# Bilinear stage of a two-layer graph network: the sixteen products of a tile stored term by term instead of value by value

## The reference, cut to what matters

```
node = h @ W1                              # h = layernorm(x), 4096x128; W1: 128x16
hw = jnp.einsum('nc,kcf->nkf', h, W2)      # W2: 16x128x128
x = jnp.einsum('nk,nkf->nf', node, hw)     # 16 terms summed, weighted per row
x = adj @ x
x = x + node @ b
return jax.nn.relu(x)
```

## Time and profile before

| what | us |
|---|---|
| runs of the kernel before, median of 3 | 2064.73 (2064.36 to 2067.2) |
| the profiled execution's own time | 2066.36 |
| its span in the trace | 2064.6 |
| the loop over the 32 tiles, from the first product to the end of the last sum | 1561.0 to 1657.2 |
| busy in the span: TensorE, VectorE, ScalarE, GpSimd | 1814.2, 1639.6, 1351.9, 203.1 |
| mean granted TensorE clock over the span | 0.921 of full speed |

### The profile page before, as it was taken

One profiled execution on the slowest core, in us unless ns is written; L12 is line 12 of the kernel. 1 busy time (PEld: TensorE's weight loads), 2 busy tenths in 40 slices (PEclk: granted clock), 3 DMA queues, 4 the chain that ended last, 5 costly groups with the idle time before them and its releaser, 6 DMA issues.

```text
span 2064.6 us, 28345 instructions
## 1 busy us (share of the span) xinstructions
PE 1814.2 (88%) x8959; PEld 877.8 (43%) x9108; DVE 1639.6 (79%) x1427; ACT 1351.9 (65%) x1498; POOL 203.1 (10%) x158
## 2 busy tenths in 40 slices
PE   1531969999999999999997999999998889997997
PEld 1521434444444444444446444444453344454443
DVE  7655669888989898989566787777858988856997
ACT  6876148887887887887244556555546877735775
POOL 0000000000101011001450000000006900000000
PEclk6555989999999999999996999999989999988999
DMA  9996066555555556455400311101002089913221
GB/s 385 411 421 223 32 204 204 152 152 173 151 151 172 152 152 180 143 153 157 170 0 1 105 52 41 51 34 47 1 21 122 0 327 428 421 44 105 102 102 62
DMA packets 94318, 309.76 MB, mean 150 GB/s; under 512 B 15513, under 2 KB 52857, under 8 KB 80399
## 3 DMA queue, kind: packets, MB, share of 16 engines
q1 hardware_dynamic: 94242, 308.79, 42.7%
HBM read 295.78 MB, written 12.98 MB: 150 GB/s over the span
## 4 chain that ended last, share of the span: by engine, by line
PE 52%; DVE 3%; ACT 2%; issue 2%; POOL 1%; ACTq 0%; DVEq 0%; POOLq 0%
PE psum L1132 13%; PE psum L1144 13%; PE psum L1217 8%; PE psum L1080 8%; PE psum L1105 1%; PE psum L1107 1%; PE psum L907 1%; PE psum L1195 1%; DVE prod L1754 1%; PE psum L1119 1%; PE psum L902 1%; PE psum L913 1%; POOL halves L577 1%; PE psum L1110 1%; PE psum L1109 1%
## 5 line engine op out<-in xcount | busy, mean ns | idle before, releaser
L733 ACT ACTIVATE ss<-KR,cls 128x1024 bf16<-128x1024 int16 x384 | 413.0, 1138 | 106.8 <-DVE pl L1589 106.4
L1080 PE MATMUL psum<-ph,Tt 128*128 128x512 bf16 x1503 | 410.9, 380 | 9.2 <-DVE pl L1589 7.5
L811 ACT ACTIVATE hid<-psum,fB 128x1024 f32<-128x1024 f32 x208 | 227.3, 1112 | 184.2 <-PE psum L1132 184.2
L1132 PE MATMUL psum<-hTp,fW 128*128 (+1 forms) x1202 | 285.2, 383 | 11.6 <-ACT hid L811 3.8
L1144 PE MATMUL psum<-hidp,fW 128*128 128x512 bf16 x1241 | 281.0, 381 | 2.4 <-DVEq L1720 2.1
L1586 DVE TENSOR_TENSOR ph<-ss,Ahi 128x3072 bf16<-128x3072 bf16 x128 | 228.5, 1785 | 54.6 <-PE psum L1080 54.5
L1698 DVE TENSOR_TENSOR hidp<-hid,hidp 128x1024 bf16<-128x1024 f32 x208 | 245.4, 1222 | 26.7 <-ACT hidp L805 26.5
L1080 PEld LDWEIGHTS psum<-ph,Tt 128*128 128x128 bf16 x1536 | 150.0, 98 | 191.0 <-DVE pl L1589 7.1
L1589 DVE TENSOR_TENSOR pl<-ss,Alo 128x3072 bf16<-128x3072 bf16 x128 | 227.2, 1775 | 0.0
L1080 PE MATMUL psum<-pl,Tt 128*128 128x512 bf16 x753 | 225.7, 380 | 0.8
L1132 PEld LDWEIGHTS psum<-hTp,fW 128*128 128x128 bf16 x1248 | 117.1, 98 | 168.9 <-ACT hid L811 32.2
(11 more groups left out here) (231 smaller groups left out, 2063.5 us busy)
## 6 DMA issues: line engine op xcount, KB each, us to landing
Ar<-in_adjT SPq DMA_DIRECT2D x64, 1024.0 KB, 11.6
Ab<-in_adjT SPq DMA_DIRECT2D x128, 512.0 KB, 4.0
A<-in_adjT SPq DMA_DIRECT2D x32, 2048.0 KB, 10.2
mB<-mk_d SPq DMA_DIRECT2D x64, 512.0 KB, 3.7
Tt<-T_d SPq DMA_DIRECT2D x128, 192.0 KB, 2.3
Tt<-Tn_d SPq DMA_DIRECT2D x128, 64.0 KB, 2.1
T_d<-tb SPq DMA_DIRECT2D x32, 192.0 KB, 1.9
RD<-rden_d SPq DMA_DIRECT2D x12, 512.0 KB, 5.1
```

Of the source, the lines that this page charges most:

```text
L733: last = nc.scalar.activation(ss[s % 2][:, h, :], KR[:, h, rb * RB:(rb + 1) * RB], ACT.Sigmoid, scale=STEP, bias=cls[:, ds(t * HEADS + h, 1)])
L811: nc.scalar.activation(hid[j % HB][:, :], flat[:, j % 2 * CW:j % 2 * CW + CW], func, bias=fB1[:, j:j + 1]).then_inc(act_done[k], 1)
L1080: last = nc.tensor.matmul(psum[:, 2 * h + q, :], Tt[s % AS][:, h, w, :], mv[:, q * CH:(q + 1) * CH], start=fresh and k == 0, stop=False, s ...
L1132: last = nc.tensor.matmul(psum[:, j % 2 * 2 + b, :], fW[0][x][:, j * P:(j + 1) * P], hTp[y][:, ds(q * CW + b * CH, CH)], start=(w == 0), s ...
```

## The change

The two tiles are laid out with k outermost and f innermost. The products of a term are written side by side, 128 values in a row (ScalarE) and 1024 in a row (VectorE); GpSimd adds two blocks of 1024 values that each lie in one piece; the last sum reads, for each f, eight values that lie 512 bytes apart. Places, sizes, semaphores, the counts of instructions and their order are as before.

```diff
-        prod = [sb(f"prod{i}", [P, P, K1], F32, 100 + 8 * i) for i in range(2)]
+        prod = [sb(f"prod{i}", [P, K1, P], F32, 100 + 8 * i) for i in range(2)]
...
-        halves = [sb(f"halves{i}", [P, P, K1 // 2], F32, 119 + 4 * i) for i in range(2)]
+        halves = [sb(f"halves{i}", [P, K1 // 2, P], F32, 119 + 4 * i) for i in range(2)]
...
-                pool.tensor_tensor(halves[s][:, :, :], prod[s][:, :, 0:K1 // 2], prod[s][:, :, K1 // 2:],
+                pool.tensor_tensor(halves[s][:, :, :], prod[s][:, 0:K1 // 2, :], prod[s][:, K1 // 2:, :],
                                    ALU.add).then_inc(b_half, 1)
...
-                        prod[s][:, :, k], psum[:, 4 * s + k // 4, k % 4 * P:k % 4 * P + P], ACT.Copy,
+                        prod[s][:, k, :], psum[:, 4 * s + k // 4, k % 4 * P:k % 4 * P + P], ACT.Copy,
...
-                V.tensor_tensor(prod[s][:, :, K1 // 2:].rearrange("p f k -> p k f"),
+                V.tensor_tensor(prod[s][:, K1 // 2:, :],
                                 psum[:, 4 * s + 2:4 * s + 4, :].rearrange("p b (k f) -> p (b k) f", f=P),
...
-                V.tensor_reduce(xf[s][:, :], halves[s][:, :, :], AX, ALU.add).then_inc(b_sum, 1)
+                V.tensor_reduce(xf[s][:, :], halves[s][:, :, :].rearrange("p k f -> p f k"), AX,
+                                ALU.add).then_inc(b_sum, 1)
```

## The result

| | before | changed |
|---|---|---|
| median of ten runs each, us | 2066.43 | 2070.66 |
| ratio of changed to before, with its 95% interval | | 1.0023 (1.0014 to 1.0032) |
| profiled execution, us (span) | 2066.36 (2064.6) | 2074.05 (2072.2) |

The changed kernel is slower: 4.2 us between the medians, a ratio of 1.0023. The interval lies above 1 and on both sides of the 0.2% that the prediction took as its limit for "no difference", so there is a small loss, but whether it passes that limit is not settled. The forecast was 2065.2 us with 0.5 us lost, in a range of 2061.5 to 2074. The time is in that range, which is 12.5 us wide; the loss is eight times the one that was forecast.

A forecast was written before the change was run, and what follows sets the result against it. VectorE was taken to bound the bilinear stage, GpSimd close behind. 31 x 0 for the loop, - 0.17 at the head and + 0.69 at the end gave plus 0.5 us: 2065.2 us against a median of 2064.73, range 2061.5 to 2074.

The forecast's parts named there:

- Who sets the pace: Bilinear stage: VectorE has no idle time and sets 2.913 us a tile; GpSimd's floor is 2.87.
- The stepped write, 0.69 us: VectorE's product, line 1754: writing side by side saves 0.69 us of 1.90 a tile.
- The stepped read, 1.90 us: VectorE's last sum, line 1762: reading at 512 bytes' distance raises it from 1.21 to 1.90 us.
- Together again 2.85: VectorE's loop, start to start: 1.05 plus 1.80 us a tile, unchanged, since the toll only moves from write to read.
- The end, plus 0.69 us: After the last halves: the longer last sum has no shorter product to pay for it, plus 0.69 us.
- The head, minus 0.17: Before the first halves, which wait for ScalarE's last activation: its side-by-side write saves 0.17 us, once.
- The signs of being wrong: Loop under 87 us, or a longer loop with both VectorE lines as forecast, meaning xf to high_x isn't covered.
- What comes after moves along and costs nothing: After the stage: copies of A and TensorE move with the last sum; TensorE's clock after its longer pause costs nothing.
- Cover for `xf`: ScalarE's high_x: the sum's extra 0.69 us fits in the 1.09 us that high_x waits behind ScalarE's own products.
- reads nearly free: Rival: the sum takes 1.45 us or less and GpSimd becomes the bound, 2063.5 or 2061.5 us; chance 0.24.
- The sum becomes the bound: Rival: VectorE's sum takes 2.29 us, plus 13.0 us, 2077.7; beyond the 0.2% band from 2.02 us; chance 0.17.
- The product doesn't get shorter: Rival: VectorE's product stays at 1.90 us and the reads cost 8 to 22 us, 2072 to 2087; chance 0.04.

The follow-up runs named there:

- e4: Only halves stored term by term (k outermost), prod left value by value, against the kernel before: 2086.10 us against 2065.03, ratio 1.0103.
- e2: Values kept in blocks of two f, written in pieces and read in steps of 8 bytes, against the kernel before: 2062.25 us against 2065.03, ratio 0.9982.
- e3: Only prod stored term by term, halves value by value, GpSimd writing in steps, against the kernel before: 2061.37 us against 2065.03, ratio 0.9986.
- e7: ScalarE's eight terms in their own tile, term by term, VectorE's still value by value, against the kernel before: 2073.41 us against 2066.27, ratio 1.0038.

## Why the prediction was right or wrong

- **The number:** in the range, and partly by luck. Plus 4.2 us were measured where 0.5 stood in the sum. The stage explains 2.1 of them, and the rest of the loss lies in a part of the kernel that the prediction left out. The range was wide enough for both.
- **Who sets the pace:** right in the main. VectorE is full before and after; e4 adds the tolls up on it, and 21 us come out. But the 0.06 us a tile that the prediction called handovers are mostly waits of the sum for GpSimd's halves: two engines shared the bound before, and only VectorE sets it after.
- **The stepped write, 0.69 us:** right as a duration (0.68), wrong as used. The step "product to sum 1.74 - 0.69 = 1.05" took the whole difference in duration from the distance between starts. The distance fell only to 1.13: the stepped product overlapped its successor by 0.16 us (1.90 - 1.74), the plain one by 0.09 (1.22 - 1.13).
- **The stepped read, 1.90 us:** right that the 64-byte write was the row to go by and not the 12-byte read. It measured 1.94, and 0.73 from start to start, not 0.69.
- **"Together again 2.85", and 31 x 0 in the sum:** this is the term that was mis-sized. 1.13 + 1.84 = 2.97 a tile, 0.12 above the sum of the prediction: 0.08 us in one distance and 0.04 in the other. About half of it came back, because the waits for GpSimd vanished. The term is best read from halves to halves, because the last product starts later behind its longer sum and is shorter by as much. From the first halves to the last it is 1658.37 - 1566.23 = 92.14 us, against 1653.58 - 1563.40 = 90.18: plus 2.0 us, where I had 0. Two tolls of 0.7 us that cancel leave a difference of their small errors, counted 31 times.
- **The end, plus 0.69 us:** right. From the last halves to line 1206 it is 1662.88 - 1658.37 = 4.51 us, against 1657.40 - 1653.58 = 3.82: plus 0.69. **The head, minus 0.17:** it gave 0.11 (first halves 2.25 us behind the first product, 2.36 before). The three measured terms add up to the stage: 1.96 + 0.69 - 0.11 = 2.54 us.
- **The signs of being wrong:** one of them came up. First to last product was to stay at 90.3 us within 1, and it took 92.9 with both VectorE lines as forecast. The prediction put this case down to the wait of high_x for `xf`. That wait stayed covered; the cause is the 0.12 us of the term above.
- **What comes after moves along and costs nothing:** wrong for the measured time. The rest takes 2.6 us more in the trace, and the clock in the next layernorm and router accounts for it. The prediction looked at the clock only where TensorE paused next to the stage, and there it gave 0.5 us back.
- **Cover for `xf`:** right. high_x still starts behind ScalarE's own products (1612.69, the sum had ended at 1612.34).
- **Rivals:** "reads nearly free" was wrong of this layout but right in its arithmetic: e2 and e3 remove the toll, GpSimd sets the pace, and 2.8 and 2.9 us are won in the loop where I had 1.3. Its floor is 2.82 and not 2.87: in the earlier trace rows line 583 starts 0.11 us behind the end of the halves, and 0.19 us behind the end of ScalarE's high_x, as far as at the marked wait of 1618.29. So GpSimd waited there unmarked; in e2 line 583 starts 0.05 us in front of the end of the halves. "The sum becomes the bound" had the right sign for another reason: the sum took 1.94 us, below the 2.02 from which that rival begins. "The product doesn't get shorter" was wrong.

## What to carry to other kernels

In these runs a float32 value that VectorE writes or reads alone in its 16 bytes costs about 0.7 to 0.8 ns extra: reads at 16 bytes of distance as at 512 (1.97 and 1.94 us per 1024 values), writes at 32 and 64 (2.02 and 1.90), against 1.22 side by side. Storing it the other way round moves the price, and storing in pairs (two values to each piece, in either direction) removes it. When two costs on the bounding engine cancel, take distances between starts and not durations, since the error counts once a tile, and look whether the second engine's waits were hidden in today's pace. If a layout must be turned, GpSimd's write side did it here for 0.02 us of 2.36. And before moving a two-input instruction to VectorE, see whether GpSimd reads SBUF all the time.

## What the runs showed that I had not expected

- GpSimd's writes in steps of 32 and 512 bytes are nearly free (2.38 us in e3 and in e4, against 2.36), the read of one input in steps of 512 bytes is not (2.89 us in e7).
- A step of 16 bytes is slightly dearer for VectorE's sum than one of 512: 1.97 against 1.94 us, 3.05 against 3.00 us a tile.
- A VectorE subtraction of 128 values took 1.69 us instead of 0.28 beside GpSimd's addition.
- The same work from line 1217 to the end takes 395.8 to 400.1 us; the 400.1 goes with a lower granted clock of TensorE in the layernorm and router (0.59 against 0.72).
